# Seventeen groups of experts placed inside the second attention of a four-layer transformer step

## The reference

```python
x = x + attn_a(layernorm(x), ...)   # 16 heads of 8; scores * tril / exp(n), no softmax; then Wo
x = x + ffn(layernorm(x), ...)      # 16 experts, top 2, capacity 1.25; silu(gate) * up, down; combined by weight
x = x + attn_b(layernorm(x), ...)   # per head: the 6 queries with the largest max score attend, others are zero
x = x + ffn(layernorm(x), ...)
```

## Time and profile before

| | |
|---|---|
| runs | 1408.18 us median of 3, 1398.48 to 1413.44 |
| profiled execution | 1396.88 us, span 1395.1 us, mean granted TensorE clock 0.936 |
| busy | PE 1239.1, weight loads 787.4, DVE 1042.0, ACT 756.4, POOL 836.4 us |
| second attention, first to last score | 503.81 to about 1130 us, 38 to 42 us a batch but for batch 0 |
| expert segments 0, 1 / 2, 3 | from about 344 to 503.8 / 1132 to 1299.5 us |

### The profile page before, as it was taken

One profiled execution on the slowest core, in us unless ns is written; L12 is line 12 of the kernel. 1 busy time (PEld: TensorE's weight loads), 2 busy tenths in 40 slices (PEclk: granted clock), 3 DMA queues, 4 the chain that ended last, 5 costly groups with the idle time before them and its releaser, 6 DMA issues.

```text
span 1395.1 us, 28372 instructions
## 1 busy us (share of the span) xinstructions
PE 1239.1 (89%) x8534; PEld 787.4 (56%) x8534; DVE 1042.0 (75%) x4462; ACT 756.4 (54%) x1901; POOL 836.4 (60%) x1246
## 2 busy tenths in 40 slices
PE   3999998996999999999999999999999999999100
PEld 1566665565898965454545445545455469888100
DVE  2899999895674458898999989989998856565322
ACT  2444444442665767666676756656676546556000
POOL 3237776777525224356777767766874445367776
PEclk9999999997999998998999989999999899999655
DMA  6845602011556520000100001011000125466522
GB/s 174 259 154 192 197 30 87 28 44 60 171 163 210 166 65 16 14 11 24 32 25 29 32 24 32 29 62 48 29 28 14 44 79 162 150 218 205 150 75 75
DMA packets 119783, 125.80 MB, mean 90 GB/s; under 512 B 15568, under 2 KB 109904, under 8 KB 119632
## 3 DMA queue, kind: packets, MB, share of 16 engines
q1 hardware_dynamic: 103248, 90.42, 20.5%
q0 software_dynamic: 16384, 33.59, 7.9%
HBM read 50.15 MB, written 73.79 MB: 89 GB/s over the span
## 4 chain that ended last, share of the span: by engine, by line
PE 70%; DVE 12%; POOL 7%; issue 4%; DMA 2%; ACT 2%; SPq 0%; POOLq 0%; ACTq 0%; DVEq 0%
PE pair L1897 25%; PE pair L1823 8%; POOL vmyg L564 6%; PE pair L1685 5%; DVE pT L1401 5%; PE bank L1709 4%; PE pair L1834 4%; PE pair L1812 2%; PE bank L1630 2%; PE bank L1624 2%; PE pair L1674 2%; DVE xs L1318 2%; PE bank L1936 1%; PE bank L1916 1%; PE pair L1695 1%
## 5 line engine op out<-in xcount | busy, mean ns | idle before, releaser
L1897 PE MATMUL pair<-kT,apart 32*128 32x512 f32 x2048 | 460.2, 672 | 3.5 <-DVE smax L1401 2.0
L1401 DVE CUSTOM_DVE_ANT_0 pT<-pair,pT 128x256 f32<-128x256 f32 x1024 | 384.2, 416 | 76.1 <-ACT pT L925 70.4
L925 ACT ACTIVATE pT<-pair 128x256 f32<-128x256 f32 x1024 | 327.0, 397 | 196.8 <-PE pair L1897 193.3
L1897 PEld LDWEIGHTS pair<-kT,apart 32*128 32x128 f32 x2048 | 192.8, 192 | 128.1 <-DVE smax L1401 78.7
L564 POOL DMA_INDIRECT vmyg<-ybufA,slg x128 | 123.7, 966 | 110.6 <-DVE smax L1401 67.9
L1823 PE MATMUL pair<-xeT,unit_w 128*128 128x256 f32 x768 | 184.6, 384 | 0.0
L564 POOL DMA_INDIRECT vmyg<-ybufB,slg x128 | 122.8, 959 | 71.3 <-DVE smax L1401 33.6
L509 POOL DMA_INDIRECT dispB<-xnf,sli x128 | 129.3, 1010 | 57.0 <-issue 35.2
L509 POOL DMA_INDIRECT dispA<-xnf,sli x128 | 130.0, 1016 | 50.9 <-issue 30.2
L1128 DVE TENSOR_TENSOR pT<-pair,causal 128x1024 f32<-128x1024 f32 x128 | 151.2, 1213 | 12.1 <-PE pair L1685 11.2
L1293 DVE TENSOR_TENSOR hid<-sg,pair 128x512 f32<-128x512 f32 x96 | 65.7, 685 | 123.3 <-ACT sg L851 123.1
(11 more groups left out here) (231 smaller groups left out, 1947.6 us busy)
## 6 DMA issues: line engine op xcount, KB each, us to landing
dispB<-zeros SPq DMA_DIRECT2D x16, 1408.0 KB
apart<-dispA SPq DMA_DIRECT2D x96, 128.0 KB
ybufA<-ye SPq DMA_DIRECT2D x48, 256.0 KB
apart<-dispB SPq DMA_DIRECT2D x96, 128.0 KB
ybufB<-ye SPq DMA_DIRECT2D x48, 256.0 KB
dispA<-zeros SPq DMA_DIRECT2D x33, 128.0 KB
xs<-in_x SPq DMA_DIRECT2D x16, 256.0 KB, 3.1
out<-xs SPq DMA_DIRECT2D x15, 256.0 KB, 2.6
```

What stands on the lines that cost most here:

```text
L925: act.activation(rel[n % RING][:, q, :], pair[n % RING][:, q, HALF:SEQ], ACT.Relu).then_inc(s["relu_done"], 1)
L1401: dve.tensor_tensor_reduce(out=rel[n % RING][:, q, :], in0=pair[n % RING][:, q, 0:HALF], in1=rel[n % RING][:, q, :], scale=1.0, scalar=LOW ...
L1897: pe.matmul(pair[n % RING][:, q, :], apart[h][at, j, t * P:(t + 1) * P], kTs[h][at, HALF:], start=True, stop=True).then_inc(s["bsc_done"], 1)
```

## The change

Segment 1's groups 13 to 23 and segment 2's groups 0 to 5 move into attention B, at most two to a batch: batches 0 to 5 and 13 to 15. The first place has its transposes at n = 1 and its gate at n = 4, the second at n = 13 and 16. Each such group takes two further slots of the ring: a "turn" slot (first half: its transposes; second half: the down product of the group before) and a "gate" slot (gate in one half, up in the other). A pair's slot is now its place in that longer sequence (`PAIR_AT`), and what a half waits for is what stood three slots back (`ring_free`). Their rows come into tiles of their own, `xw`, of which there are two, and POOL copies all their weights, one batch ahead. Batch 0's queries and keys, and one of two additions and norms, are moved earlier in segment 1 or into batch 0 (`start_b`, `body`), and the routing of the last batch in segment 2 is pressed into 18 groups. Not shown are the same steps in shared functions (`expert_x`, `expert_silu`, `expert_hidden`, `expert_y`, `expert_turn`, `expert_in`, `expert_down`), which are those of before with the group's number over all segments, k.

```diff
+M1 = 13
+M2 = 6
+PLACES = ((1, 4), (13, 16))
...
+for _b in range(B):
+    for _n in range(PAIRS):
+        PAIR_AT[_b * PAIRS + _n] = len(RING_OF)
+        RING_OF.append(("pair", _b * PAIRS + _n))
+        for _k, _p, _p2 in WITHIN.get(_b, ()):
+            if _n == _p:
+                TURN_AT[_k] = len(RING_OF)
+                RING_OF.append(("turn", _k))
+            if _n == _p2:
+                GATE_AT[_k] = len(RING_OF)
+                RING_OF.append(("gate", _k))
+        if (_b, _n) == TAIL:
+            TAIL_AT = len(RING_OF)
+            RING_OF.append(("tail", 2 * GRP))
...
@@ SP: load, and the order of loads and stores
+                if k in GATE_AT:
+                    into = xw[g % 2]
+                    if k - 2 in GATE_AT:
+                        sp.wait_ge(s["xe_tp"], k - 1)
...
+            for g in range(M1, GRP):
+                if g + 2 < GRP:
+                    load(1, g + 2)
+                store(1, g - 1)
...
+            for g in range(M2):
+                if g + 2 < M2:
+                    load(2, g + 2)
+                if g:
+                    store(2, g - 1)
+            for g in range(M2, M2 + NX):
+                load(2, g)
+            store(2, M2 - 1)
+            experts(2, M2)
@@ POOL: body, before the last two sends; and the start
+                for k, _, _ in WITHIN.get(b + 1, ()):
+                    copies(k // GRP, k % GRP)
...
             norm_scale(CALLS, TB)
             normed(0, B, xnb[0], "att", 0, CALLS)
+            fetch(1, 1, range(TB, TB * K))
+            for k, _, _ in WITHIN[0]:
+                copies(k // GRP, k % GRP)
+            key_differences(0, 0)
             norm_scale(CALLS + 1, TB)
@@ ACT: body
+                    for k in gated_in(b, n):
+                        expert_silu(k, pair[GATE_AT[k] % RING][:, 0, :])
+                    for k in turned_in(b, n - 1):
+                        expert_x(k, pair[TURN_AT[k] % RING][:, 0, :])
@@ DVE: body, and the steps of segment 2
+                    for k in turned_in(b, n):
+                        if k != 2 * GRP:
+                            expert_y(k - 1, pair[TURN_AT[k] % RING][:, 1, :])
...
+                    for k in gated_in(b, n - 1):
+                        dve.wait_ge(s["up_done"], GATED.index(k) + 1)
+                        expert_hidden(k, pair[GATE_AT[k] % RING][:, 1, :])
+                    if not last and n == 0:
+                        add_first(1, 1)
+                    if not last and n == 1:
+                        add_second(1, 1)
...
+                if g == 13:
+                    route_max(b + B, bank[0])
                 if g == 14:
-                    route_max(b + B, bank[0])
+                    route_top(b + B)
                 if g == 15:
-                    route_top(b + B)
+                    route_ranks(b + B, bank[0])
+                    table_counts(3, bank[0])
@@ PE: start of attention B, ring, body; ranks of the last batch at step 14 (16 before)
+            experts(1, start_b, stop=M1)
+            project_k(0)
+            pe.wait_ge(s["hid_done"], GRP + M1)
+            pe.wait_ge(s["y_ready"], GRP + M1)
...
+            def ring_free(r, q):
+
+                if r < RING:
+                    return
+                what, k = RING_OF[r - RING]
+                if what == "pair":
+                    pe.wait_ge(s["bmax_done"], 2 * k + q + 1)
+                elif what == "gate" and q == 0:
+                    pe.wait_ge(s["silu_done"], k + 1)
+                elif what == "gate":
+                    pe.wait_ge(s["hid_done"], k + 1)
+                elif q == 0:
+                    if what == "turn":
+                        pe.wait_ge(s["xeT_ready"], k + 1)
+                else:
+                    pe.wait_ge(s["y_ready"], k + 1)
...
                 for n in range(PAIRS):
-                    scores(b, h, n, not last)
+                    scores(b, h, n)
+                    for k in turned_in(b, n):
+                        down_beside(k - 1, TURN_AT[k])
+                    if (b, n) == TAIL:
+                        down_beside(2 * GRP - 1, TAIL_AT)
+                    for k in turned_in(b, n - 1):
+                        turn_beside(k)
+                    for k in gated_in(b, n):
+                        gate_beside(k)
+                    for k in gated_in(b, n - 1):
+                        up_beside(k)
```

More of the change, by code:

```diff
@@ L684, in body @@
             def body(b, u, h, x, last=True, next=True, fetch_=True, before=True):
-                if not next:
-                    for g in range(NX):
-                        copies(2, g)
                 def pair_made(n):
@@ L724, in body @@
                     normed(b + 2, b + 2 + B, xnb[(x + 2) % 4], "att", 0, att_call(b + 2))
+                for k, _, _ in WITHIN.get(b + 1, ()):
+                    copies(k // GRP, k % GRP)
+                if not next:
+                    copies(2, M2)
+                    copies(2, M2 + 1)
                 send_tile(26, 2)
@@ L860, in copies @@
                     last.then_inc(s["unit_w_act"], 1)
-                xT(0)
-                for g in range(G):
-                    if g + 1 < G:
+                xT(first)
+                for g in range(first, stop):
+                    if g + 1 < stop:
                         xT(g + 1)
                     silu(g)
-                    if 2 <= g < G - 2:
+                    if g + 2 < stop and base + g + 2 not in POOL_COPIED:
                         copies(g + 2, weights_of(mybir.EngineType.Activation, seg, g + 2, 1))
                     if pieces:
-                        pieces(g)
+                        pieces(g - first)
             def chain_a(g):
@@ L984, in pieces @@
                     turned(2 * B - 1, "ffn", xfT)
-                if g == 14:
                     route_exp(2 * B - 1)
-            experts(2, pieces)
+            experts(2, pieces, first=M2)
             experts(3)
@@ L1799, in _, with expert_turn, expert_in, expert_ready @@
             values(B - 1, 1, TB - 1)
-            def experts(seg, pieces=None):
-                base, G = seg * GRP, GRP
+            def expert_turn(k, src, dst):
+                pe.wait_ge(s[f"xe_in{k % NX}"], (k // NX + 1) * 16 * GU)
+                for j in range(GT):
+                    last = pe.transpose(dst[:, j * P:(j + 1) * P], src[:, j, :], ident[:, :])
+                last.then_inc(s["xe_tp"], 1)
+            def expert_in(k, part, dst):
+                for u in range(GU):
+                    last = pe.matmul(dst[:, u * UR:(u + 1) * UR], unit_w[k % NX][:, u, part * D:(part + 1) * D],
+                                     xeT[k % 2][:, UT * u:UT * (u + 1), :].rearrange("p j n -> p (j n)"), start=True, stop=True)
+                return last
+            def expert_ready(k):
+                pe.wait_ge(s["xeT_ready"], k + 1)
+                pe.wait_ge(s["unit_w_ready"], pool_copies(k))
+                if act_copies(k):
+                    pe.wait_ge(s["unit_w_act"], act_copies(k))
+            def expert_down(k, dst):
+                pe.wait_ge(s["hid_done"], k + 1)
+                for j in range(GT):
+                    last = pe.matmul(dst[:, j * D:(j + 1) * D], hid[k % 2][:, j, :], unit_w[k % NX][:, j // UT, 2 * D:3 * D],
+                                     start=True, stop=True)
+                last.then_inc(s["y_done"], 1)
+            def experts(seg, pieces=None, first=0, stop=GRP):
+                base = seg * GRP
                 if seg == 0:
@@ L1845, in experts @@
                     if pieces:
-                        pieces(g)
-                down(G - 1)
+                        pieces(g - first)
+                if stop == GRP:
+                    down(GRP - 1)
             def chain_a(g):
@@ L1973, in body @@
                         turn_largest(b - 1, 1 - h)
-                    if next and n == 7:
+                    if next and n == q_at - 2:
                         if last:
```

274 lines of the change are left out of this document (154 added, 120 removed).

## The result

The changed kernel takes 1465.8 us (median) against 1404.6 for the one before: ratio of the runs 1.0398, 95% interval 1.0294 to 1.0502, so **slower by 4%**. The forecast said slower, and gave 1438 with a range up to 1456: the sign is right, the size is not. The profiled execution took 1452.0 us against 1396.9 (span 1450.1 against 1395.1), so 55 of the 61 us can be looked up in the two traces.

What follows compares the result with a forecast made beforehand. TensorE was taken to bound the kernel, in the second attention taking scores and other work strictly in turn, VectorE nearly full too. From 1396.9 us, -33.4 + 3.5 + 68.7 - 1 = +37.8 gave 1434.7, put at 1438; range 1402 to 1456.

Steps and rivals of the forecast that it cites:

- Earlier start: Before the second attention: first scores stand near 470.4 instead of 503.81, -33.4 us.
- Work moved into batch 0: Batch 0 of the second attention: the second batch's two additions and statistics on VectorE cost +3.5 us, bounds 1 to 4.
- First place 3.9, second 4.2: Second attention: each group's cost in us by its place in a batch; nine first and eight second places, +68.7.
- ScalarE's two passes at nothing: Second attention: a moved group's two ScalarE passes fall in that engine's idle third, at no cost.
- That the last down and copy in batch 5 "and the missing ones in batch 13 cancel": Second attention: segment 1's last down and copy add 1.1 us in batch 5, cancelled by those missing in batch 13.
- Batch 15 taken as the others: Last attention batch: its one group counted as a first place like the other eight, 3.9 us.
- End: Segment 2: six groups fewer save only 1 us, the last batch's sends being near to bounding it; bounds -6 to +3.
- Rival C: Segment 2's end: the last batch's chain shortens with the groups, -18.4 instead of -1; 1417 to 1420 us; chance 0.08.
- From the profiled sum to the median: Whole kernel: from 1434.7 us in a profile to a forecast of 1438; runs lie up to 17 above.
- B: Nine attention batches' score gaps: TensorE has room, only VectorE pays; 1382 us, or 1365 with the end paying; chance 0.14.
- D: Second attention: neighbouring pairs still run together, a group costs 2.3 us; no measurable change, 1405 to 1411; chance 0.18.

Runs made afterwards that it cites:

- none_spread: Changed kernel with no group moved and segment 2's routing steps and sends put back where the kernel before has them: 1408.2 us, 1.0037.
- run 6: Kernel before, no group moved, with TensorE's four pieces alone added at the seventeen places, on other data, without slots or ScalarE and VectorE passes: 1478.0 us, 1.0528.
- second_only: Changed kernel with only segment 2's six groups inside the attention (M1 = 24): 1439.6 us, 1.0245.
- no_table: Changed kernel with ScalarE's silu of the moved groups replaced by a plain copy, so no table loads for them: 1451.9 us, 1.0342.
- fill: Changed kernel with four transposes and two 512-column matmuls of other data added in batch 15: 1447.3 us, 1.0340.
- the first experiments: Each half of the change alone: only segment 1's eleven groups inside the attention (1440.5 us), or only segment 2's six (1439.6 us).
- first_only: Changed kernel with only segment 1's eleven groups inside the attention (M2 = 0), packed routing steps kept: 1440.5 us, 1.0256.
- late_places: Changed kernel with the groups at pairs 6 and 9, and 20 and 23, instead of 1 and 4, and 13 and 16: 1472.1 us, 1.0472.
- slots_only: Changed kernel with none of the moved groups' matmuls inside the attention and no table loads; slots, waits and other passes kept: 1452.0 us, 1.0328.

## Why the prediction was right in sign and wrong in size

The sum missed the profiled execution by 17.3 us, and most of that is one step: each group's price was summed at full clock, and batch 15 got 34 us at half clock (+11.6). The median then lay 13.8 above the profiled execution where the prediction allowed 3.3. Smaller terms had no cost or the wrong one: the table loads, and the group boundary in batch 5. Term by term:

- *Earlier start, -33.4:* right, -34.4, by the mechanism given. (The prediction's own terms, 467.7 and 3.0, add up to 470.7 rather than 470.4; measured was 470.08.)
- *Work moved into batch 0, +3.5:* too much, as far as it can be read. In none_spread batches 0 and 1 together are 1.6 longer, with 20.5 us at half clock in the two where before had 18.5.
- *First place 3.9, second 4.2:* right as far as they went, 3.8 and 3.9 in batch 4, for the reason given: serial steps of 1.06 us, which run 6 alone reproduces.
- *ScalarE's two passes at nothing:* **failed.** The cover named, ScalarE's idle third, is true of the passes, but not of the table loads that silu brings with it. 14 loads were added; where one stands ahead of the exponentials it costs the batch 1.1, and 7 of the 14 stand so: an estimate of some 8 us. The first place's load was covered. This hides in the batch terms of the sum: the 8.7 measured in batch 4 for 8.1 forecast is 7.6 + 1.1.
- *That the last down and copy in batch 5 "and the missing ones in batch 13 cancel":* **failed**, +4.3. Batch 13's first place costs 3.8 by pair 6 with nothing to bring down; why it isn't cheaper was not tested. In batch 5 the lone down and copy cost 1.4 by pair 20; 0.8 followed at pair 21, and the rest with 6.8 us at half clock near the end.
- *Batch 15 taken as the others:* **failed**, +11.6, the largest miss in the profiled execution. The price was summed at full clock for all nine batches. Before, batch 15 had 6.8 us at half clock; now there are 34, which take 17 us of TensorE by estimate. The fall is there in both traces of the changed kernel, but second_only and no_table have only 10.2 us of it in the same batch, so what makes the rest stays open. Batch 0 is another such place: its first place costs 11.0 instead of 3.9, with 17.1 us at half clock, and only by the rest being cheaper is the batch near its forecast (12.3 for 11.6). That too is luck: in run fill, the same kernel up to batch 15, batch 0 is 7.1 longer, with 6.8 us at half clock.
- *End, -1:* the number is right (-0.1 from the last score pass to the end), but by luck, since its reason is half of it. I had "the sends are near to bounding this end"; the runs show packed steps that cost 14 and six groups that give 12.7 back. Bounds of -6 to +3 for it held. Rival C was closer in mechanism than its 0.08 said.
- *From the profiled sum to the median, +3.3:* **failed.** 1434.7 was for an execution like the profiled one; the text itself said that the median before lay 11.3 above. Three executions of the changed kernel in the result go from 1452.0 at a mean clock of 0.923 to 1466.0 at 0.913; those of the kernel before beside the first experiments go from 1397.7 at 0.932 to 1409.3 at 0.921.

Start -1.0, batch 15 +11.6, batch 5 +4.3, end +0.9, the other batches together +1.3: 17 of the 17.3 us by which the profiled execution misses 1434.7. The rest of the gap to 1465.8 is 13.8 of the median above the profile, for which 3.3 was allowed. That batches 6 to 12 differ by only 0.3 in all is luck as well: in first_only, whose code is the same up to batch 11, batches 10 and 11 alone are 10.4 longer than before, with 37 us at half clock.

The rivals: B is out (a group's pieces alone cost over 70 us in all), D is out (late_places), C is half right.

No run made a version that beats the kernel before. The price shows why: a group costs 3.06 us in the expert stage; in the attention of the changed kernel a first place cost 3.3 to 4.6 at full clock (batches 1 to 4, 13 and 14, by pair 6), and the other places tried were no cheaper.

## What to carry to other kernels

Before you move work between two stages, ask in both whether the busy engine works in turn. Here it did, and the full pieces were paid about in full: 7.5 us of TensorE for two groups, and with the pieces alone 6.5 lost in batch 2 and 7.8 in batch 4 by pair 20. Cost the table that each ScalarE function needs, not only its pass. Where TensorE sets the pace, take both levels of its clock into the range. And trace a kernel more than once before you read a few us in one batch: batch 4 of the same code took 8.7 us more than before in one trace and 17.0 in another.

## What the runs showed that I had not expected

Leaving out work can cost as much as it saves. slots_only has 339 fewer TensorE matmuls in the attention than the changed kernel (3058 against 3397), and in its profiled execution, the longest of its four, takes 713.9 us for it against 713.0, at a mean clock of 0.86 against 0.94.

The clock also falls in different places in executions of the same code. Up to batch 11, first_only is the changed kernel. Its batch 4 is 17.0 longer than before instead of 8.7, with 20.5 us at half clock where the changed kernel's trace has none; its batches 10 and 11, which hold no moved group, have 37 us at half clock where that trace has 3.4.

What exactly makes the clock fall is not settled. Batch 15 kept most of its clock without table loads and without filler (0.90), also in second_only, which has the loads (0.90), and lost it with the pieces alone (0.66).
